# A two-layer attention and expert network on one core: a longer ring of probabilities, three single buffers, and the gate's scaling on VectorE

## The reference, cut to what matters

```python
x = L0_attn_x                                   # (2, 1024, 128), float32
xn = _layernorm(x)
s = _L0_attn_ref(xn, ...)                       # 16 heads of 8, rotary, causal
g = _silu(_L0_ffn_ref(xn, ...))                 # soft mixture of 8 experts x 64 slots
x = x + s * g
xn = _layernorm(x)
s = _L1_attn_ref(xn, ...)
g = _silu(_L1_ffn_ref(xn, ...))                 # 16 experts, top 2, each takes 512 tokens
x = x + s * g
return x
# attention:  softmax(mask(rope(q) @ rope(k).T * D ** -0.5)) @ v, then @ w_out + b_out
# _L1_ffn_ref ends:  z = xn + outs;  (z - mu) / sqrt(var + 1e-5) * gamma + beta
```

## Time and profile before

| | |
|---|---|
| median of 3 runs | 696.48 us (693.71 to 697.3) |
| the profiled execution | 697.95 us |
| its span, first to last instruction | 696.2 us |
| TensorE busy | 615.2 us (88%), weight loads 286.5 us |
| DVE busy | 508.5 us (73%) |
| ACT busy | 453.4 us (65%) |
| POOL busy | 260.8 us (37%) |
| TensorE's mean granted clock | 0.969 of full speed |
| chain that ended last | PE 63%, POOL 9%, DVE 8%, ACT 7%, issue 6%, DMA 3% |

### The profile page before, as it was taken

How to read it: one execution, slowest core, us unless ns; L and a number is a source line. 1 busy time by engine, 2 the same in 40 slices (tenths; PEclk the granted TensorE clock), 3 DMA queues, 4 the chain that set the end, 5 groups by cost and what they waited for, 6 DMA issues and landing times.

```text
span 696.2 us, 14421 instructions
## 1 busy us (share of the span) xinstructions
PE 615.2 (88%) x4988; PEld 286.5 (41%) x5052; DVE 508.5 (73%) x829; ACT 453.4 (65%) x904; POOL 260.8 (37%) x459
## 2 busy tenths in 40 slices
PE   0679889959999999999999998998999999899954
PEld 0446657323553345443343443423333233347522
DVE  7969365838686887799898878989989889733303
ACT  1375575647668777787767768676776778782751
POOL 5566820011020217574311267712113112125883
PEclk9889999988999999999999999999999999999986
DMA  5055834040130303052422430534123023000002
GB/s 179 0 172 146 254 122 154 2 100 1 32 70 32 72 30 93 9 159 85 125 54 63 157 83 9 161 121 102 45 56 87 26 59 69 3 1 1 1 1 60
DMA packets 36013, 52.12 MB, mean 75 GB/s; under 512 B 5992, under 2 KB 27400, under 8 KB 33672
## 3 DMA queue, kind: packets, MB, share of 16 engines
q1 hardware_dynamic: 33264, 50.48, 26.3%
q10 hardware_dynamic: 2680, 0.73, 0.5%
HBM read 37.29 MB, written 13.63 MB: 73 GB/s over the span
## 4 chain that ended last, share of the span: by engine, by line
PE 63%; POOL 9%; DVE 8%; ACT 7%; issue 6%; DMA 3%; ACTq 2%; another core or an unknown queue 1%; POOLq 0%; SPq 0%; DVEq 0%
PE ps L1336 58%; ACT probs L1049 3%; PE ps L1555 2%; DMA qop<-shiftT 2%; POOL gate L571 2%; ACTq L1062 2%; DVE maxes L1320 1%; DVE sine L1179 1%; POOL gate L922 1%; POOL F L916 1%; POOL gate L923 1%; DMA F<-in_w 1%; DVE bnst L1090 1%; POOL xn L571 1%; ACT F L987 1%
## 5 line engine op out<-in xcount | busy, mean ns | idle before, releaser
L1320 DVE TENSOR_REDUCE maxes<-ps 128x2 f32<-128x1024 f32 (+3 forms) x292 | 340.4, 1206 | 69.0 <-PE ps L1336 66.0
L1049 ACT ACTIVATE probs<-ps 128x512 f32<-128x512 f32 x576 | 305.4, 604 | 106.6 <-PE ps L1336 78.9
L877 POOL TENSOR_SCALAR_AFFINE_SELECT probs<-probs 128x512 f32<-128x512 f32 (+1 forms) x160 | 83.8, 548 | 247.3 <-ACT probs L1049 246.8
L1336 PE MATMUL ps<-qop,kop 128*128 128x512 bf16 (+3 forms) x704 | 161.1, 327 | 14.1 <-ACT probs L1049 8.7
L1336 PE MATMUL ps<-probs,vals 128*9 128x512 f32 (+3 forms) x1536 | 155.7, 496 | 7.9 <-POOL probs L877 6.1
L1336 PE MATMUL ps<-kmx,qmx 32*128 32x128 bf16 (+2 forms) x1280 | 104.0, 263 | 9.8 <-DMA qop<-shiftT 7.2
L1336 PEld LDWEIGHTS ps<-qop,kop 128*128 128x128 bf16 x768 | 58.9, 99 | 103.0 <-ACT probs L1049 52.4
L1336 PEld LDWEIGHTS ps<-kmx,qmx 32*128 32x128 bf16 x1280 | 39.0, 92 | 112.7 <-issue 70.4
L1336 PE MATMUL ps<-F 128*128 128x128 f32 (+2 forms) x640 | 73.9, 278 | 3.7 <-ACT F L987 2.7
L1336 PEld LDWEIGHTS ps<-F 128*128 128x128 f32 (+2 forms) x640 | 66.4, 176 | 19.6 <-issue 13.8
L1336 PEld LDWEIGHTS ps<-probs,vals 128*9 128x9 f32 x1536 | 27.0, 89 | 64.6 <-issue 49.1
(11 more groups left out here) (158 smaller groups left out, 635.8 us busy)
## 6 DMA issues: line engine op xcount, KB each, us to landing
qop<-q_thirds SPq DMA_DIRECT2D x42, 192.0 KB
kop<-k_thirds SPq DMA_DIRECT2D x42, 192.0 KB
F<-in_w SPq DMA_DIRECT2D x16, 256.0 KB, 3.9
qmx<-q_thirds SPq DMA_DIRECT2D x14, 256.0 KB
kmx<-k_thirds SPq DMA_DIRECT2D x14, 256.0 KB
q_thirds<-third SPq DMA_DIRECT2D x8, 384.0 KB, 4.4
k_thirds<-third SPq DMA_DIRECT2D x8, 384.0 KB, 3.3
q_thirds<-third SPq DMA_DIRECT2D x8, 256.0 KB, 3.3
```

The source lines that it names most:

```text
L877: last = pool.affine_select(where, where, [[0, number], [1, P]], ALU.is_ge, 0.0, base=0, channel_multiplier=-1)
L1049: act.activation(probs[:, u % RING, :], bank(at), ACT.Exp, scale=SCALE).then_inc(s_cells_read, 1)
L1320: dve.tensor_reduce(dst, src, AX.X, ALU.max).then_inc(s_units_read[pair // 2], 1)
L1336: return pe.matmul(out_, lhsT, rhs, start=first, stop=last)
```

## The change

- `RING` is 36 // 2 = 18: the exponentials may run 18 units ahead of the sums over values, for 12.
- `sine`, `attT` and `shiftH` have one buffer each, and `F`, whose top was not used, is 256 columns shorter. `qk` of the key (n = 1) now waits for the `sum` of the query of the same quarter, `qk` of the query for the key's `sum` of the quarter before; `attT` c waits for `proj` c - 1; the second part of a split `shift` waits for the DMA of the first.
- `sum` of layer 1 moves from POOL to DVE. `lnroot` and `ln` move from POOL to DVE; the semaphore between `lnstat` and `lnroot` goes, as both are now on one engine.
- The DMAs of `shift` are issued by SP (queue of the loads) instead of ACT (a queue that carried nothing else after the start), behind a wait for ACT's copy.
- The planner's numbers follow: prices of `shift`, `ln`, `lnroot` and `sum`; a bank of ring A is taken as free after its first reader; all offsets of `MORE` and the bonuses of `STAY` are others. So the order of all engines is another one, and the diff doesn't show it.

```diff
-RING = NU // 3
+RING = NU // 2
...
-STAY = {"whole": 46.0, "rows": 28.0, "columns": -13.0, "halves": 10.0, None: 0.0}
+STAY = {"whole": 110.0, "rows": -5.0, "columns": -4.0, "halves": 10.0, None: 0.0}
...
-    "add": (159, -76), "attT": (-5, -103), "colsum": 125, "comb": 160, "count": -120, "ct": 160, "diag": -57, "disp": 83,
...
+    "add": (147, -34), "attT": (43, 160), "colsum": 104, "count": 150, "ct": 125, "diag": -99, "disp": -118, "emb": -72,
...
-    ... "shift": (0.15, "A", (("ACT", 0.3),)) ...
+    ... "shift": (0.15, "A", (("ACT", 0.3), ("SP", 0.7))) ...
-    ... "lnroot": (0, "", (("POOL", 2.4),)), "ln": (0, "", (("POOL", 1.6),)) ...
+    ... "lnroot": (0, "", (("DVE", 2.4),)), "ln": (0, "", (("DVE", 1.0),)) ...
...
-        return 0, "", (("POOL", 1.27) if arg[0] else ("DVE", 0.62),)
+        return 0, "", (("DVE", 0.62),)
...
-            [("exp", n - 1, FIRST_UNIT[1])] if n else [])
+            [("exp", n, 0)] if c == 1 else [("exp", n - 1, FIRST_UNIT[1])] if n else [])
...
-        return [("heads", L, c // 2, c % 2)] + ([("proj",) + divmod(4 * L + c - 2, 4)] if L or c >= 2 else [])
+        return [("heads", L, c // 2, c % 2)] + ([("proj",) + divmod(4 * L + c - 1, 4)] if L or c else [])
...
-        sine = sb("sine", [P, 2, BANK])
+        sine = sb("sine", [P, BANK])
-        attT = sb("attT", [P, 2, BANK])
+        attT = sb("attT", [P, BANK])
-        shiftH = sb("shiftH", [2 * HG, 2, BANK], BF16)
+        shiftH = sb("shiftH", [2 * HG, BANK], BF16)
-        F = sb("F", [P, 9984])
+        F = sb("F", [P, 9728])
...
+                elif kind == "shift":
+                    n, part = arg
+                    sp.wait_ge(s_cells_read, CELL[what] + 1)
+                    if part == 2:
+                        for k in range(2):
+                            sp.dma_start(qop[KR + k:KR + k + 1, n % 2, :, :], shiftT[HG * TB * k:HG * TB * k + HG * TB, :]
+                                         ).then_inc(s_shift_in[k][n % 2], 16)
+                    else:
+                        sp.dma_start(qop[KR:KR + 2, n % 2, :, BANK * part:BANK * part + BANK], shiftH[:, :]
+                                     ).then_inc(s_shift_in[part][n % 2], 16)
...
-                        act.wait_ge(s_cells_read, CELL[what] + 1)
-                        for k in range(2):
-                            act.dma_start(qop[KR + k:KR + k + 1, r, :, :], shiftT[HG * TB * k:HG * TB * k + HG * TB, :]
-                                          ).then_inc(s_shift_in[k][r], 16)
...
-                    own.link(normalise(pool, gate, gate, mv, root[:, 0, 1, :], range(t, t + 1)))
-                    own.link(pool.tensor_tensor(gate[:, t, :], gate[:, t, :], gam1, ALU.mult))
-                    pool.tensor_tensor(gate[:, t, :], gate[:, t, :], bet1, ALU.add).then_inc(s_ln, 1)
...
+                    own.link(normalise(dve, gate, gate, mv, root[:, 0, 1, :], range(t, t + 1)))
+                    own.link(dve.tensor_tensor(gate[:, t, :], gate[:, t, :], gam1, ALU.mult))
+                    dve.tensor_tensor(gate[:, t, :], gate[:, t, :], bet1, ALU.add).then_inc(s_ln, 1)
...
+                    own.link(refine(dve, own, *(root[:, 0, n, 4 * c:4 * c + 4] for n in range(3))))
```

More of the change, by code:

```diff
@@ L150 @@
 MORE = {
[L151 to L160 removed]
+    "add": (147, -34), "attT": (43, 160), "colsum": 104, "count": 150, "ct": 125, "diag": -99, "disp": -118, "emb": -72,
+    "embT": -109, "embstat": -96, "eo": 118, "es": -56, "exp": (-79, -106), "halve": (-21, 62), "heads": (-42, -120),
+    "hid": -64, "hid1": -116, "high": (44, 124, 85), "ldexp": (73, 94), "ldf1": 87, "ldmax": (-10, 100), "ldw": 65,
+    "ldwA": 103, "ldwB": 117, "left": (4, -22, 69), "lg": -115, "limit": 2, "ln": -23, "lnroot": -86, "lnstat": -109,
+    "logit": 145, "low": (82, 121, -9), "lt": -14, "mask": (-75, 33), "max": (-2, 72), "middle": (-107, -57, 100),
+    "mix": -66, "norm": (46, -26, 134), "offs": 144, "out": (-42, -8), "proj": (150, -120), "pv": (-113, -120),
+    "pvout": (-109, 3), "qk": (27, 139, 157), "rT": 29, "rden": (129, 114), "res": 139, "root": (102, -57), "routes": 22,
+    "rs": 72, "shift": (29, -23), "silu": (57, 148), "slot": -106, "soft": 53, "stat": (39, -72, 0), "store": (132, 97, 3),
+    "sum": (-45, 78, 101), "top": (128, -15), "total": -56, "v": (-46, -37, 32), "wg": -8, "xT": (150, 80, 160), "xr": -86,
+    "xrT": 160, "z": -111,
 }
@@ L523, in schedule @@
             tiling = shape
+        read = None
         for engine, us in takers:
             clock[engine] = end = max(clock[engine], end + HOP if pe else end) + us
+            read = read or end
         if ring:
             held[what] = len(rings[ring])
-            rings[ring].append(math.inf if kind in LATER else end)
+            rings[ring].append(math.inf if kind in LATER else read)
         elif kind in LATER.values():
@@ L546 @@
         UNIT[what] = len(UNIT)
-    same = 2 if what[0] == "sum" else 1
-    NTH[what] = 1 + sum(w[:same] == what[:same] for w in NTH)
+    NTH[what] = 1 + sum(w[0] == what[0] for w in NTH)
 def summed(n, step):
@@ L835, in _ @@
                 kind, arg = what[0], what[1:]
-                if kind == "sum" and arg[0]:
+                if kind == "left":
                     L, c, n = arg
[L838 to L843, removed]
+                    pool.wait_ge(s_summed, NTH["sum", L, c, n])
                     pool.wait_ge(s_high, NTH["high", L, c, n])
@@ L1032, in _ @@
                     act.wait_ge(s_bv, 16)
-                    act.activation(attT[:, c % 2, :], bank(at), ACT.Identity, bias=bv[:, arg[0]:arg[0] + 1]).then_inc(s_cells_read, 1)
+                    act.activation(attT[:, :], bank(at), ACT.Identity, bias=bv[:, arg[0]:arg[0] + 1]).then_inc(s_cells_read, 1)
                 elif kind == "es":
@@ L1178, in _ @@
                     for src, dst in ((slice(half, P), slice(0, half)), (slice(0, half), slice(half, P))):
-                        last = dve.scalar_tensor_tensor(sine[dst, n, :], ps[src, pair, :], bqk[src, n:n + 1],
+                        last = dve.scalar_tensor_tensor(sine[dst, :], ps[src, pair, :], bqk[src, n:n + 1],
                                                         rot[src, 1, span], ALU.add, ALU.mult)
                     last.then_inc(s_units_read[pair // 2], 1)
-                elif kind == "sum" and not arg[0]:
+                elif kind == "sum":
                     L, c, n = arg
@@ L1450, in _ @@
                     for k in range(4):
-                        last = mm(quarter(pair, k), attT[:, c % 2, P * k:P * k + P], wp[:, :])
+                        last = mm(quarter(pair, k), attT[:, P * k:P * k + P], wp[:, :])
                     last.then_inc(s_units_full, 1)
```

41 lines of the change are left out of this document (19 added, 22 removed).

## The result

The changed kernel takes 673.77 us (673.22 to 676.67) against 695.13 us (693.71 to 697.3) of the kernel before in the same comparison: a ratio of 0.9699 with an interval of 0.9657 to 0.974. It is 3.0% faster. The forecast was 682 with a range of 668 to 699: the sign and the range held, and the gain was 8 us larger than the sum. The profiled execution took 673.67 us, its span 671.9 us, 24.3 us less than the span of 696.2 before.

What follows compares the result with a forecast made beforehand. TensorE was taken as the bound in the middle (95%, DVE close at 86%), neither at the end. -8 + 1.5 - 2 + 0 - 4 + 1 - 3 = -14.5 gave 683.4, forecast as 682 from the median; range 668 to 699.

Steps and rivals of the forecast that it cites:

- The end, -8: Last stage: gate's refinement and scaling on DVE end near 665 for 675.6; 8 us less, bounds -2 and -12.
- Sums of layer 1, +1.5: Layer 1's eight sums on DVE instead of POOL: 1.5 us more, bounds 0 and +5.5.
- The shift's issue off ACT, -2: Shift DMAs issued by SP free ACT, which mostly absorbs them: 2 us less, bounds -5 and 0.
- The stall near 150 us, 0: TensorE's 6.06 us wait for a shift DMA issued behind six loads: no change, bounds -8 and +11.
- shift late behind the loads: Rival, 13%: on SP the shift waits behind loads and SP's other waits; two such stalls give 704 us, slower than before.
- The ring, -4: Ring of 18 in the attention: more `pv` steps join, fewer changes of shape; 4 us less, bounds -17 and 0.
- The rival in which the ring pays in full: Rival, 15%: most `pv` steps run in pairs, -17 us instead of -4, giving 669 us.
- The order, -3: New order of all steps leaves more exponentials to cover the last quarters: 3 us less, bounds -8 and +8.
- the single buffers, +1: Single `attT`: transposes take turns with `proj`, adding copies and hand-overs at three or four places; +1 us, bounds 0 and +3.
- Signs named ahead: Expected in the profile after: gate's end, idle time at the end, shift waits and landings, `pv` steps following without a unit between.

Runs made afterwards that it cites:

- the `ldexp` edit: Kernel before, shift still issued by ACT, with only the loads `ldexp` of group 2 placed behind `shift` of group 1 in the order: 695.87 us, ratio 1.0011.
- the fastest kernel here: Kernel before with order and ring of 12, scaling on DVE, shift on SP, `ldexp` of groups 2 and 8 behind the shifts of groups 1 and 7: 671.84 us.
- the two edits: In before's order, `ldexp` of group 2 behind `shift` of group 1 and both of group 8 behind group 7's; with scaling on DVE, shift on SP: 671.84 us.

## Why the prediction was right, and where its sum was short

**That the range held is partly luck.** Of the seven terms the end was right and the sums lay within their bounds. Two were sized far too low (ACT's issues and the stall near 150 us). The ring's -4 has nothing behind it in the runs, and it made up for a part of what those two lacked. The order's -3 and the single buffers' +1 can't be read apart.

**The end, -8: right.** The runs give 7.3 in before's order and 9.7 in after's. The steps held in three of the four quarters: refinement 2.35 us for 2.5, a tile 0.90 for 0.97, the masks no longer behind the scaling. In the fourth the refinement took 5.45 us, because POOL's products and masks fell beside it. That cost little: ACT, which takes the gate next, had waited 0.37 us for it. The prediction named ACT's exponentials as next to be late. In after they aren't: what remains are 2.42 us for ACT's copy `attT`, which stands in ACT's order behind the work on the gate, and 1.34 for POOL's `heads`. That the gate is ready 6 us ahead of the forecast 665 is the new order's doing, where the first `z` comes at 609.8 for 626.5; in before's order it was ready at 669.6.

**Sums of layer 1, +1.5: within its bounds.** Measured 0 to 1.

**The shift's issue off ACT, -2: under-sized.** It is 6.8 in after's order and about 6 in before's, beyond the bound of 5. The step that failed is "elsewhere ACT, busy at 73%, absorbs it". I had counted the two waits of TensorE that the list named (1.20 and 0.65 us). But 14 shifts at 1.3 us each are 18 us of ACT's time, and a third of that comes through, as later exponentials and not as a wait with the shift's name on it.

**The stall near 150 us, 0: the price was there, the turn it took was missed.** Its end gives about 9 us with the clock, a little beyond the bound of -8. I had the price (6.06 us and 5 of clock) and the cause (six loads just ahead), and left the sign open since the diff doesn't show the order. It also stood under the wrong heading. I tied it to the move of the issue to SP, but in after's order it is gone with the shift on ACT as well, because group 0's last exponential unit comes 10 us later and holds the loads back. In before's order neither edit alone helps: the shift on SP makes it worse (9.16 us), and the `ldexp` edit does nothing (0 us). Both together end it, since on one queue the list decides which goes first.

**The rival "shift late behind the loads": real, and not met.** The shift on SP in before's order is it: 9.16 and 5.36 us of waits and the whole relief of ACT lost. The forecast priced each such place at 11 us (6.06 and 5 of clock). Near 371 us and near 354 us it cost 5.7 and 6.5 us, little more than half. My argument against it, that the planner places the shift ahead of the next group's load, doesn't hold for before's list: of the 14 whole shifts those of groups 1 and 7 stand behind that load, and these are the two places. In after's list all 14 stand ahead of it. In after the longest landing is 5.8 us, a little over the 5 that I had named, and TensorE waits for none. The Trainium skill's rule (DMA: Bandwidth & Descriptors, "Queues, rings and completion order") is borne out in its direction: 11.7 us to landing in one ring with the loads, 9.8 from a queue of its own. Its size is small here: the queue of its own saved 2 of 11.7 us, and being ahead of the loads saved 8 to 10.

**The ring, -4: the mechanism isn't there.** The named sign was fewer changes of shape. Counted over TensorE's records (maxima, sums over values, all else) there are 716 after and 707 before; pairs of `pv` steps that stand directly together in TensorE's order are 8 for 5, of 160 steps. The longer ring is used (61 of 160 steps run with more than 12 units ahead, at most 18), but it doesn't join steps, and a kernel with ring 12 reaches 671.84. The rival in which the ring pays in full landed near the measured time, 669, by a mechanism that isn't there. This shows that the gain doesn't need the ring of 18; whether 18 gives anything with before's own order, or on top of the fastest kernel here, wasn't tried and stays open.

**The order, -3, and the single buffers, +1.** The order's reason, more exponentials left to cover the end, wasn't tested by a run of its own. What the runs do show of it is the stall near 150 us, about 9 us, which the term for the shift's queue was meant to hold. Against that the first 100 us lost 4.4 us of TensorE, which no term had. Compared with the kernel that has the scaling, the shift on SP and the two edits in before's order (670.1 in span), the new order, ring and single buffers together are 1.8 us slower, and by the medians nothing clear.

**The sum again, with what was measured.** Taken back one at a time from after, the scaling is worth 9.7 us and ACT's relief 6.8, 16.5 of the 24.3 in spans. The other 7.8 belong to the new order with ring and single buffers: about 9 for the stall near 150 us (as sized in before's order), less what the start lost, and a rest that no run takes apart. In before's order the scaling is worth 7.3, the relief about 6 and the stall about 9. They interact, since the shift on SP gives nothing where it goes behind the loads, so the terms hold only for these two sets.

**Signs named ahead:** the gate ended at 658.5 for "near 665 or earlier", idle time in the last 46 us 10.6 for "less than 12", no waits for `qop<-shiftT`, a clock of 1.00 in the middle, DVE at 86%. The longest landing, 5.8 us, missed its sign of 5. Steps of `pv` in a row and fewer changes of shape didn't come, and these are the signs that told the ring's term wrong.

## What to carry to other kernels

In this kernel a DMA issue on ACT cost it the wait for its copy's end and the issue itself, and the list of waits didn't name it. Price such an issue by its full length (here 1.3 us, of which a third came through) and check it with the drift between two traces of the same order. A small transfer that work waits for should go out ahead of the large loads. On one queue the list says which is first. On two queues it is decided by what each of them waits for, so look at when the loads are released (here 142.0 us in one order and 151.8 in the other), and not only at who issues. Where a planner's offsets are changed along with a size, undo the size with the old offsets as well as with the new ones; here the ring of 12 looks 41 us worse with the new offsets, and no worse with the old ones and two edits of the order.

## What the runs showed of the hardware

DVE's small instructions are hit hard while POOL works on large tiles. In the last quarter of after five of the twelve small instructions of the refinement take 0.49 to 1.21 us, for 0.16 to 0.17 elsewhere, the longest two beside POOL's two instructions of 1.27 us:

```profile
650.48 1.27 POOL L916 TENSOR_TENSOR gate<-gate,xn 128x512 f32<-128x512 f32 x1
651.83 1.27 POOL L917 TENSOR_TENSOR x<-x,gate 128x512 f32<-128x512 f32 x1
```

```profile
650.56 1.21 DVE L561 TENSOR_TENSOR root<-root 128x4 f32<-128x4 f32 x1
651.80 0.17 DVE L562 TENSOR_SCALAR root<-root 128x4 f32<-128x4 f32 x1
652.01 1.12 DVE L563 TENSOR_TENSOR root<-root 128x4 f32<-128x4 f32 x1
```

An instruction of 4 columns waits until POOL's whole instruction is over (650.56 + 1.21 is 651.77, POOL's ends at 651.75). All five began after an instruction of POOL had begun, and each ended 0.01 to 0.03 us after POOL's did, so here it is a lock and not a slower pace. It is the lock that the prediction drew on. The form makes no difference among these: `tensor_tensor` and `tensor_scalar` (L562, 0.49 us beside one mask) are both held. The 0.17 us at 651.80 are no exception, as that instruction began between POOL's two, 0.03 us ahead of the second. I had priced such company at a factor of 1.75; for the shortest ones it is over 7, bounded by the length of POOL's instruction. The refinement took 5.45 us in all for 2.35.
